# Gated products of expert tiles: halves turned by a crossbar DMA transpose, up products in two pairs of banks

## The reference

```python
logits = jnp.einsum('btd,de->bte', X, Wg) + bg
topv, topi = jax.lax.top_k(logits, S)          # S = 2 of 8 experts
w = jax.nn.softmax(topv, axis=-1)
xs = X[:, :, None, :] * w[..., None]
out = X
for e in range(E):
    h = jax.nn.silu(jnp.einsum('btsd,dh->btsh', xs, W1[e])) * jnp.einsum('btsd,dh->btsh', xs, W3[e])
    y = jnp.einsum('btsh,hd->btsd', h, W2[e])  # H = 512
    mask = (topi == e)[..., None]
    out = out + jnp.where(mask, y, 0.0).sum(axis=2)
```

## Time and profile before

| | |
|---|---|
| runs | 1001.63, 1004.79, 1005.98 us |
| profiled execution, span | 1000.9 us |
| busy share | TensorE 90%, VectorE 79%, GpSimd 73%, ScalarE 67% |
| weight loads of TensorE (beside matmuls) | 64% |
| mean granted clock of TensorE | 0.978 of full |
| mixtures | first about 360 to 520 us, second about 836 to 990 us |
| DMA engines | 34 GB/s over the span |

### The profile page before, as it was taken

One profiled execution on the slowest core, in us unless ns is written; L12 is line 12 of the kernel. 1 busy time (PEld: TensorE's weight loads), 2 busy tenths in 40 slices (PEclk: granted clock), 3 DMA queues, 4 the chain that ended last, 5 costly groups with the idle time before them and its releaser, 6 DMA issues.

```text
span 1000.9 us, 33897 instructions
## 1 busy us (share of the span) xinstructions
PE 897.1 (90%) x13160; PEld 640.5 (64%) x13160; DVE 792.1 (79%) x2394; ACT 673.5 (67%) x1183; POOL 734.7 (73%) x685
## 2 busy tenths in 40 slices
PE   5789999999999879899987899999999985998884
PEld 3467676776777656566654676777677764666663
DVE  6889898888889877777656889888888887866563
ACT  6688888878877626556555787767767762545552
POOL 6789989889887745666545999878888883666662
PEclk9999999999999979999999999999999997999997
DMA  5201011010030001122111000000000001121222
GB/s 153 78 10 45 3 45 45 3 45 2 3 107 3 2 20 39 52 43 85 38 30 51 3 3 3 12 3 2 13 3 3 13 2 30 41 43 44 86 62 82
DMA packets 21118, 33.79 MB, mean 34 GB/s; under 512 B 4578, under 2 KB 10466, under 8 KB 20964
## 3 DMA queue, kind: packets, MB, share of 16 engines
q1 hardware_dynamic: 13728, 18.50, 5.9%
q0 software_dynamic: 5888, 12.07, 4.8%
q10 hardware_dynamic: 1348, 1.05, 0.3%
HBM read 22.44 MB, written 9.18 MB: 32 GB/s over the span
## 4 chain that ended last, share of the span: by engine, by line
PE 63%; DVE 18%; ACT 6%; issue 6%; POOL 3%; another core or an unknown queue 2%; DMA 1%; SPq 0%; POOLq 0%; DVEq 0%; ACTq 0%
PE ps L1698 8%; PE ps L1889 8%; PE ps L1700 8%; PE ps L1699 7%; DVE arena L1308 4%; PE ps L1919 3%; PE ps L2128 3%; PE ps L1853 3%; PE ps L1920 3%; PE ps L1921 3%; PE ps L2140 2%; PE ps L2141 2%; PE ps L2142 2%; PE ps L1864 2%
## 5 line engine op out<-in xcount | busy, mean ns | idle before, releaser
L784 POOL TENSOR_TENSOR arena<-arena 128x1024 f16<-128x1024 f32 x190 | 344.9, 1816 | 86.2 <-ACT arena L980 75.9
L1308 DVE CUSTOM_DVE_ANT_0 arena<-ps,mask_qk 128x512 bf16<-128x512 f32 (+3 forms) x512 | 224.4, 485 | 25.0 <-PE ps L1853 23.8
L972 ACT ACTIVATE arena<-ps,lift 128x1024 f32<-128x1024 f32 (+1 forms) x192 | 186.7, 972 | 85.0 <-PE ps L1899 82.2
L1889 PE MATMUL ps<-arena 64*128 64x512 f16 (+3 forms) x1536 | 148.5, 299 | 10.2 <-ACT arena L972 6.8
L835 POOL DMA_INDIRECT arena<-x_rows,arena x92 | 92.6, 1006 | 88.5 <-PE ps L2103 43.7
L1919 PE MATMUL ps<-arena 128*128 128x65 f16 x1280 | 130.9, 195 | 0.2 <-DVE arena L1332 0.2
L1920 PE MATMUL ps<-arena 128*128 128x64 f16 x1280 | 130.4, 193 | 0.0
L1921 PE MATMUL ps<-arena 128*128 128x65 f16 x1280 | 130.0, 194 | 0.0
L843 POOL DMA_INDIRECT y_rows<-arena x92 | 90.8, 987 | 49.0 <-ACT arena L1138 26.1
L1919 PEld LDWEIGHTS ps<-arena 128*128 128x128 f16 x1280 | 117.4, 98 | 8.4 <-issue 0.5
L1920 PEld LDWEIGHTS ps<-arena 128*128 128x128 f16 x1280 | 117.9, 99 | 0.2 <-issue 0.2
(11 more groups left out here) (288 smaller groups left out, 2695.9 us busy)
## 6 DMA issues: line engine op xcount, KB each, us to landing
stage<-in_L_ffn_W SPq DMA_DIRECT2D x4, 1024.0 KB, 5.3
arena<-y_rows SPq DMA_DIRECT2D x14, 256.0 KB, 3.6
x_rows<-XN SPq DMA_DIRECT2D x8, 256.0 KB, 2.1
arena<-x_rows,arena POOLq DMA_INDIRECT x92
y_rows<-arena POOLq DMA_INDIRECT x92
stage<-in_L_attn_Wkv SPq DMA_DIRECT2D x2, 512.0 KB, 8.3
X<-in_L_attn_tokens SPq DMA_DIRECT2D x3, 256.0 KB, 5.1
out_x<-X SPq DMA_DIRECT2D x3, 256.0 KB
```

Of the source, the lines that this page charges most:

```text
L784: g.tensor_tensor(PL[:, b, :, cols], P32[:, :, cols], PH[:, b, :, cols], ALU.subtract).then_inc(s_pl, 1)
L972: a_.activation(P32[:, :, UNIT_AT[u]:UNIT_AT[u] + UNIT_W[u]], ps[:, 4:6, 0:UNIT_W[u]], ACT.Exp, bias=lift[:]).then_inc(s_ex_p, 1)
L1308: v_.tensor_tensor_reduce(masked[:, x, 0:w], ps[:, 2 + x, at:at + w], mask_qk[:, CH - w:CH], 1.0, NEG, ALU.add, ALU.max, accum_out=MX[:, i ...
L1889: mm(ps[:, 4 + x, at:at + w], keys, queries, start=(n_ == 0 and part == 0), stop=False)
```

## The change

Up products of tile t go to banks 1 and 2 for even t and 3 and 4 for odd t, and wait for the readers of tile t - 2. The four transposes on TensorE go. ScalarE casts the high half of the product straight from `G32` and VectorE subtracts the low half, both in SBUF, into one of three buffers `GS` (128 x 1024 of 16 bits: high half, then low half). In the queues of ScalarE and VectorE this now stands ahead of the gate and of the product of the tile behind. SP waits for the low half and for the down product that last used the target, and issues one transposing DMA, which writes the eight turned 128 x 128 blocks to one of four buffers `GT`. Down reads `GT` with a lag of 4 instead of 3 and waits for this DMA, and the scatter follows nine steps behind the gather instead of eight. SP's other transfers get places between the transposes, and in the attentions, by step.

```diff
--- before.py
+++ after.py
@@ -140,7 +140,8 @@
 
 
         ARENA = 22320
-        GRING = 3
+        GRING = 4
+        SRING = 3
         XRING = 4
         YRING = 4
         arena = sb("arena", [P, ARENA], F32)
@@ -230,9 +231,9 @@
         XG = carve([XRING, D], F32)
         XTt = carve([2, 2, P], F16)
         SA = carve([2, H], F32)
-        GL = carve([GRING, HB, P], F16)
         G32 = carve([2, H], F32)
-        GH = carve([GRING, HB, P], F16)
+        GS = carve([SRING, 2, H], F16)
+        GT = carve([GRING, 2, HB, P], F16)
 
         ps = ctx.enter_context(nc.psum_tensor("ps", [P, 8, CH], F32))
 
@@ -370,7 +371,7 @@
         s_b_ps = sem("b_ps")
         s_a_sb = sem("a_sb")
         s_g32_rdy = sem("g32_rdy")
-        s_gt_ps = sem("gt_ps")
+        s_g_turned = [sem("g_turned0"), sem("g_turned1"), sem("g_turned2"), sem("g_turned3")]
         s_g_hi = sem("g_hi")
         s_g_lo = sem("g_lo")
         s_y_ps = sem("y_ps")
@@ -529,16 +530,20 @@
         UNIT_W = (CH, CH, 2 * P)
         KEY_AT = {k: UNIT_AT[u] + at for u, unit in enumerate(EXP_UNITS) for k, at in unit}
 
-        TLAGS = (0, 1, 2, 3)
-        OUT_LAG = 8
+        DOWN_LAG = 4
+        OUT_LAG = 9
 
         def run_tiles(m, stages, carried):
 
-            for t in range(ETILES + TLAGS[-1]):
-                for f, lag in zip(stages, TLAGS):
-                    if f is not None and 0 <= t - lag < ETILES:
+            for t in range(ETILES + DOWN_LAG):
+                for f, lag in stages:
+                    if 0 <= t - lag < ETILES:
                         f(t - lag, ETILES * m + t - lag)
                 carried(m, t)
+
+        def up_banks(t):
+
+            return 1 + 2 * (t % 2), 2 + 2 * (t % 2)
 
         def second_weights(i):
 
@@ -586,10 +593,46 @@
...
+            def results_in(m, h):
+
+                for k in range(YRING):
+                    sp.wait_ge(s_y_out[k], moved(m, k, HT * (h + 1)))
+                for c in range(HCH * h, HCH * (h + 1)):
+                    for j in range(TOPK):
+                        at = j * TOK + c * CH
+                        sp.dma_start(Yt[:, c, j], y_rows[at:at + CH].rearrange("(p t) d -> p t d", t=TPC)
+                                     ).then_inc(s_y_got[c], 16)
...
+            def attention(a):
+
+                def body(t):
+                    if a == 0 and t == 0:
+                        expert_block(0)
+                    if a == 0 and t == 1:
+                        expert_block(1)
+                    if a == 0 and t in (6, 10, 14, 18):
+                        expert_block((t - 6) // 4 + 2)
+                    if a == 0 and t == 27:
+                        second_layer()
+                    if t in ROWS_OUT[a]:
+                        rows_out(*ROWS_OUT[a][t])
+                run_items(body, range(TURNS))
+
+            ROWS_OUT = ({20: (3, 0), 28: (3, 1)}, {13: (5, 0), 21: (5, 1), 29: (5, 2)})
@@ -603,34 +646,41 @@
...
+            def moe(m):
+
+                for t in range(ETILES):
+                    w = ETILES * m + t
+                    sp.wait_ge(s_g_lo, w + 1)
+                    if t >= GRING:
+                        sp.wait_ge(s_y_ps, w - GRING + 1)
+                    sp.dma_start_transpose(GT[:, t % GRING].rearrange("p k f d -> p (k f) d"),
+                                           GS[:, t % SRING].rearrange("p k h -> p (k h)")
+                                           ).then_inc(s_g_turned[t % GRING], 16)
+                    if m == 0 and t == 4:
+                        rows_out(3, 2)
+                    if m == 0 and t == 7:
+                        rows_out(3, 3)
+                    if m == 1 and t == 0:
+                        rows_out(5, 3)
+                    if t == 31:
+                        results_in(m, 0)
+                    if m == 1 and t == 38:
+                        stored(0)
+                    if m == 1 and t == 41:
+                        stored(1)
+            attention(0)
+            moe(0)
+            results_in(0, 1)
+            attention(1)
+            moe(1)
             end_loads()
@@ -1121,14 +1171,14 @@
                     act.wait_ge(s_a_ps, w + 1)
                     if t >= 2:
                         act.wait_ge(s_g32_rdy, w - 1)
-                    a_.activation(SA[:, t % 2, :], ps[:, 1, :], ACT.Silu, scale=wup[:, t:t + 1]).then_inc(s_a_sb, 1)
+                    a_.activation(SA[:, t % 2, :], ps[:, up_banks(t)[0], :], ACT.Silu, scale=wup[:, t:t + 1]
+                                  ).then_inc(s_a_sb, 1)
 
                 def product_high(t, w):
-                    act.wait_ge(s_gt_ps, w + 1)
-                    if t >= GRING:
-                        act.wait_ge(s_y_ps, w - GRING + 1)
-                    a_.activation(GH[:, t % GRING].rearrange("p a b -> p (a b)"), ps[:, 3 + t % 2, :], ACT.Copy
-                                  ).then_inc(s_g_hi, 1)
+                    act.wait_ge(s_g32_rdy, w + 1)
+                    if t >= SRING:
+                        act.wait_ge(s_g_turned[(t - SRING) % GRING], moved(m, (t - SRING) % GRING, t - SRING + 1))
+                    a_.activation(GS[:, t % SRING, 0], G32[:, t % 2, :], ACT.Copy).then_inc(s_g_hi, 1)
 
                 def result(t, w):
                     k = t % YRING
@@ -1136,7 +1186,7 @@
                     if t >= YRING:
                         act.wait_ge(s_y_out[k], moved(m, k, t))
                     a_.activation(YS[:, k, :], ps[:, 5, 0:D], ACT.Copy, scale=0.5 / W_UP).then_inc(s_y_sb, 1)
-                run_tiles(m, (token_high, gate, product_high, result), carried)
+                run_tiles(m, ((token_high, 0), (product_high, 2), (gate, 1), (result, DOWN_LAG)), carried)
 
             attention(0)
             moe(0)
@@ -1658,16 +1708,15 @@
                     dve.wait_ge(s_a_sb, w + 1)
                     dve.wait_ge(s_b_ps, w + 1)
                     if t >= 2:
-                        dve.wait_ge(s_gt_ps, w - 1)
-                    v_.scalar_tensor_tensor(G32[:, t % 2, :], ps[:, 2, :], wup[:, t:t + 1], SA[:, t % 2, :], ALU.mult,
+                        dve.wait_ge(s_g_hi, w - 1)
+                    v_.scalar_tensor_tensor(G32[:, t % 2, :], ps[:, up_banks(t)[1], :], wup[:, t:t + 1], SA[:, t % 2, :], ALU.mult,
                                             ALU.mult).then_inc(s_g32_rdy, 1)
 
                 def product_low(t, w):
-                    g = t % GRING
                     dve.wait_ge(s_g_hi, w + 1)
-                    v_.tensor_tensor(GL[:, g].rearrange("p a b -> p (a b)"), ps[:, 3 + t % 2, :],
-                                     GH[:, g].rearrange("p a b -> p (a b)"), ALU.subtract).then_inc(s_g_lo, 1)
-                run_tiles(m, (token_low, product, product_low, None), carried)
+                    v_.tensor_tensor(GS[:, t % SRING, 1], G32[:, t % 2, :], GS[:, t % SRING, 0], ALU.subtract
+                                     ).then_inc(s_g_lo, 1)
+                run_tiles(m, ((token_low, 0), (product_low, 2), (product, 1)), carried)
 
             attention(0)
             moe(0)
@@ -2105,13 +2154,14 @@
                 def up(t, w):
                     k, e = t % 2, offsets[t]
                     pe.wait_ge(s_t_lo, w + 1)
-                    if t >= 1:
-                        pe.wait_ge(s_a_sb, w)
-                    split_mm(ps[:, 1, :], XTt[:, k, 0], XTt[:, k, 1], E1h[:].rearrange("p e h -> p (e h)")[:, ds(e, H)],
+                    a_bank, b_bank = up_banks(t)
+                    if t >= 2:
+                        pe.wait_ge(s_a_sb, w - 1)
+                    split_mm(ps[:, a_bank, :], XTt[:, k, 0], XTt[:, k, 1], E1h[:].rearrange("p e h -> p (e h)")[:, ds(e, H)],
                              E1l[:].rearrange("p e h -> p (e h)")[:, ds(e, H)], s_a_ps)
-                    if t >= 1:
-                        pe.wait_ge(s_g32_rdy, w)
-                    split_mm(ps[:, 2, :], XTt[:, k, 0], XTt[:, k, 1], E3h[:].rearrange("p e h -> p (e h)")[:, ds(e, H)],
+                    if t >= 2:
+                        pe.wait_ge(s_g32_rdy, w - 1)
+                    split_mm(ps[:, b_bank, :], XTt[:, k, 0], XTt[:, k, 1], E3h[:].rearrange("p e h -> p (e h)")[:, ds(e, H)],
                              E3l[:].rearrange("p e h -> p (e h)")[:, ds(e, H)], s_b_ps)
                     if t % HT % 8 == 5 and t % HT + 3 < HT:
                         load_offsets(t + 3)
@@ -2119,29 +2169,20 @@
                         pe.wait_ge(s_r_tile, PARTS * m + 2)
                         load_offsets(HT)
 
-                def turned_product(t, w):
-                    k = t % 2
-                    pe.wait_ge(s_g32_rdy, w + 1)
-                    if t >= 2:
-                        pe.wait_ge(s_g_lo, w - 1)
-                    for f in range(HB):
-                        ins_ = nc.tensor.transpose(ps[:, 3 + k, f * P:(f + 1) * P], G32[:, k, f * P:(f + 1) * P], ident[:])
-                    ins_.then_inc(s_gt_ps, 1)
-
                 def down(t, w):
                     g, e = t % GRING, offsets[t]
```

(10 more changed lines are left out.)

45 lines of the change are left out of this document (16 added, 29 removed).

## The result

The kernel after takes 1013.29 us, the median of five runs (1012.03 to 1015.65), beside 1005.98 us for before in the same comparison. The ratio is 1.0085, with a 95% interval of 1.0057 to 1.0113: slower by 0.85%, where 968 us and a gain of 3.7% were forecast. The profiled execution has a span of 1011.0 us.

What follows compares the result with a forecast made beforehand. It took TensorE's 2.52 us a tile plus 0.57 us of waiting as the bound, with GpSimd's 2.56 next. Terms -23 - 18 - 5 + 6.5 + 3 + 2 = -34.5 us gave 966.4 from 1000.9, put at 968 us; range 943 to 1010.

Steps and rivals of the forecast that it cites:

- TensorE's part: Expert stages: removing four transposes and two waits cuts TensorE's own time per tile from 2.52 to 2.08 us.
- The transfer: Crossbar transpose on SP's queue, one per tile: 3.8 us from low half to landing, with ends of 2.1 and 9.0.
- hidden while two steps are longer than latency + 0.55: Cover of the transposing DMA before the down product: at 3.8 us latency, hidden from 2.18 us a step.
- The new step: Steady tiles: second stage bound by GpSimd's 2.56 and TensorE's 2.43 us, 23 us less; first stage at 2.55, 18 less.
- Rival B: Expert stages: ScalarE's holds stay uncovered, TensorE keeps all 0.57 us, 2.65 us a tile, about 983 us; chance 0.14.
- The ends: End of each expert stage: nothing covers the longer chain, 3.3 us more, twice, 6.5 us in all.
- The tiles outside the steady parts: 25 tiles before and after the steady stretches lose 0.44 us of TensorE each; half counted, 5 us less.
- SP's queue: Sorted-result loads stand ahead of transposes 32: 1.5 us more in each expert stage, 3 us.
- the statistics: GpSimd's statistics step for the second layer: ScalarE's normalization at step 40 waits for it, 2 us more.
- Rival D: Expert stages: latency near 5.2 us, step 2.9 us, gains lost at ends and on SP, 1000 to 1008 us; chance 0.07.
- Rival C: Expert stages: the transfer is the bound, deciding from 5.6 us latency; at 9.0 us some 1175 us; chance 0.19.
- Rival E: TensorE's granted clock in the expert stages: a mean of 0.92 would cost up to 16 us, 985 us; chance 0.05.

Runs made afterwards that it cites:

- third group: After unchanged, beside three cut-down kernels of before, on the chip where before takes 967.2 us: after took 972.21 us.
- its twins: Before with the scatters of the results left out, on the chip where before takes 967 us: 965.70 and 966.08 us.
- slack kernel: After with one more step between token and up product, down lag 5, two banks for results and turned tokens: 1018.03 us (ratio 1.0107 to before), later 1025.36 us.
- second group: Before and after run again unchanged, beside two changed kernels, on a chip where before takes 1008.21 us: before 1008.81 us, after 1015.68 us, ratio 1.0079.
- its twin: After with the extra step between token and up product, down lag 5 and doubled banks, also without the scatters of the results: 968.66 us.

## Why the prediction was wrong

**TensorE's part: right.** 2.08 us a tile was forecast, and 2.08 us is what undisturbed tiles take in the third group.

**The transfer: shorter than estimated, its spread left out.** From the end of the low half to the landing 3.8 us were estimated. In the trace SP issues a transfer 0.03 us after the low half, and it lands a median of 3.2 us later (of the 70 landings that can be read). But a tenth of them take 4.8 us or more, and two right behind the loads of sorted results took 7.6 and 7.9 in the third group. SP needs 1.2 us to issue one, not the 0.43 of a plain transfer:

```profile
L664 SPq DMA_TRANSPOSE arena<-arena x92: 885/1233/2573, 375.2 to 994.3; - x92
```

The condition "hidden while two steps are longer than latency + 0.55" is met by the median at (3.2 + 0.55) / 2 = 1.9 us a step, and by a latency of 4.8 us only from 2.7 us. What the failures cost is told by the waits: 4.8 us in 868 to 980 us of after, three times, and 7.2 us in 850 to 935 us of the third group, four times. That such a wait comes back is an argument from the program: ScalarE, in order, waits for the result of the same down product before it makes the halves of a later tile, whose transfer starts late in turn.

The Trainium skill, "VectorE: DVE Perf Modes" (section "The three transpose paths"), gives the 1309 ns for one 128 x 128. Read as a price of each block it fails here: eight blocks in one transfer took 3.2 us, not 10.5; one block alone was in no run. The rate of the Trainium skill, "DMA: Bandwidth & Descriptors" (section "Latency and other measured facts"), by which 256 KB would be an estimated 1.0 us, is nearer: the transposes' packets come to 2242 us in all, and 2242 / 16 / 92 is 1.5 us of all sixteen engines a transfer.

**The new step: this is what failed.** The prediction took the waiting in before (0.57 us a tile) for something TensorE suffers and GpSimd, at 2.56 us, would hide, and put the new step just over the later of two bounds, at 2.6 us. Two things speak against it.

First, 2.6 us was about right where nothing is late, but before goes as fast there. After's pace is 2.75 us, of which the one step behind the loads of sorted results makes 0.13; without it the mean is 2.62, GpSimd's own 2.6. Before, whose TensorE needs 2.52, went at 2.64, by its twins. With transposes alone 2.60 was left, with scatters alone 2.60, with neither 2.30. The gain was limited to nothing by that alone.

Second, the late increments come on top of that pace, and aren't hidden behind GpSimd: its gathers wait for the increment of the token transpose. In 868 to 980 us of before it waited 14.3 us for line 2103, and 9.0 us more with a releaser that the trace can't name, which the prediction didn't count: 23.3 us. In after it waits 12.8 + 10.9 = 23.7 us, though this wait was to be gone. So before goes from 2.64 to 3.09 and after from 2.75 to 3.16, 0.45 and 0.41 us a tile for the late increments. Rival B, that TensorE keeps all 0.57, was the right kind of case, but it too had them replace GpSimd's bound and not stand on it.

So TensorE's waiting grew by a little more than its work shrank: pace less undisturbed tile is 3.09 - 2.52 = 0.57 us in before and 3.16 - 2.08 = 1.08 in after.

A possible reason is the slack between two down products: in before 1.85 us lie between the end of one down product and the next (2.52 - 0.67), in after 1.41. An increment 1.73 us late with 0.5 us of copy behind it would have been covered for the most part; now 0.85 us of it is TensorE's, as at 918.93. This is an argument from the trace. The slack kernel, meant to prove it, didn't regain anything, so it isn't shown that this wait is what costs. Why more slack doesn't cover the late increments stays open.

**The other terms.** The ends were forecast at +3.3 us each and are +2.3 and +2.1: right kind, a third too large. The tiles outside the steady parts gained 1.8 and 2.3 us up to the ninth token, 4.1 together for the 5 forecast. SP's queue and the statistics (3 + 2 us) can't be told apart in the traces of the result; where nothing is late, the loads of sorted results cost the second stage up to 4.5 us, for the 1.5 counted. Forgotten was what comes after the first stage: the granted clock of 528 to 545 us is 0.65 where before has 0.90, behind an end in which TensorE was busy 16.9 of 23 us (502 to 525) where before has 19.8 of 24. Of the +3.4 us between the stages 1.9 have come about by the time the second attention is under way, none while it runs, and 1.5 between its end and the first token of the second stage. How much of it is the clock isn't shown.

**The rivals and chances.** Rival D (it does what it says and nothing comes of it, 1000 to 1008 us) comes nearest, at 0.07; its cause, a latency of 5.2 us, isn't the one found. Rival C has the pace over 3 us and TensorE waiting ahead of the down product, but it asks for a latency of 5.6 us, and most of the named waiting there is for ScalarE's copy. The time lies above the range of 943 to 1010 us, where 0.20 stood for slower, on C and the rest of D.

Rival E, the clock, came true in a small part, and no run takes it away. The mean is 0.95 and 0.98 in the two stretches where before has 0.98 and 1.00, and "1.00 through both stages" failed. In the second it is one stretch of 3.4 us at the lower level of 1.2 GHz, after 8 us in which TensorE was busy 4.88:

```profile
887.00:895.00 8.00, 4.88 (x39) 2.96 (x37) 5.24 (x20) 3.03 (x7) 5.08 (x7) 1.00 0.45 107
895.10:898.50 3.40, 3.40 (x16) 1.73 (x15) 1.57 (x3) 1.83 (x4) 2.75 (x3) 0.50 1.01 133
```

At half speed it can cost 1.7 us at most (an estimate: half of 3.4), next to the 16 us that TensorE's 0.44 us are in 36 tiles; but the 36 tiles took only 2.2 us longer than in before, and it may be much of these. The prediction's reading that the clock of before fell at 519.97 is wrong: the windows of before have 1.00 from 519.97 to 523.40 and 0.50 from 508.90 to 512.20.

The reason that nothing comes of the saving lay in the earlier trace rows: with GpSimd at 2.56 us next to TensorE's 2.52, no saving on TensorE could show in a stretch where GpSimd has work for every tile. I had that bound and took the difference to 3.09 for gain.

## What to carry to other kernels

Before an engine's work is cut, take its waiting apart from its work. Here the second bound (2.56 us beside 2.52) held for the undisturbed pace, and the disturbance, which delays both engines, stayed on top of it, 0.45 and 0.41 us a tile. The undisturbed paces had no distance, and nothing was gained. And a median latency that fits its cover can still miss it: one transfer in ten took 4.8 us or more where the median was 3.2, and the one behind other loads 7.9. The wait of a follower is to be counted whole, with the part whose releaser the trace can't name.

## What was not expected of the hardware

- The same kernel takes 967 us on one chip and 1004 to 1010 on three others. There is no lower clock behind it (0.978 mean granted against 0.973 to 0.980). By the traces of its twins without scatters, since before itself has none on the faster chip, the difference is in the expert stages alone.
- There, TensorE's semaphore increments come in bunches up to 4.1 us after the modelled ends of their matmuls in after. Of 33 bunches between 868 and 980 us of before (second group; two or more increments over 0.3 us late, within 0.15 us) 29 came 1.3 to 2.0 us after the start of a scatter; of 19 in after (same group and window) ten. A gather starts some 1.3 us ahead of each scatter, so this doesn't part the two. Without scatters the lateness is at most 0.8 us and 0.05 to 0.06 us in the mean (second stage), on two such chips, with 57 us between the slack kernel and its twin. What in the chip does this stays open.
- A transposing transfer of 128 x 1024 values of 16 bits: 1.23 us to issue, 3.2 us from issue to landing, packets of 256 B at 18 ns.
